# Scores in the free columns of the key banks, and a new order of stages, in an attention and feed-forward layer on one core

## The reference, cut to what matters

```python
h = layernorm(x) * (1 + ca) + sa                      # ca, sa, ga, sb, cb, gb come from a small matmul per sequence
q, k, v, g = h @ Wq.T, h @ Wk.T, h @ Wv.T, h @ Wg.T   # 8 heads; q, k 64 wide, v 128 wide, g 1024 wide
q, k = rotary(q), rotary(k)
o = (q @ k.T / 8 * decay[h] * causal) @ v             # decay[h] = gamma_h ** (t - s)
o = groupnorm_per_head(o) * gn_weight + gn_bias
x = x + ga * ((o * silu(g)) @ Wo.T)
h = layernorm(x) * (1 + cb) + sb
xr, xk = mixes of h with h one token before
x = x + gb * sigmoid(xr @ W_r.T) * (relu(xk @ W_k.T) ** 2 @ W_v.T)
```

## Time and profile before

| | us |
|---|---|
| median of three runs | 788.58 |
| the profiled execution | 789.72 |
| its span, first to last instruction | 787.8 |
| PE matmul busy | 753.8 (96%) |
| DVE, POOL, ACT busy | 597.4, 591.9, 443.1 |
| one group of four steps in the middle | 45.6 |

### The profile page before, as it was taken

How to read it: one execution, slowest core, us unless ns; L and a number is a source line. 1 busy time by engine, 2 the same in 40 slices (tenths; PEclk the granted TensorE clock), 3 DMA queues, 4 the chain that set the end, 5 groups by cost and what they waited for, 6 DMA issues and landing times.

```text
span 787.8 us, 29020 instructions
## 1 busy us (share of the span) xinstructions
PE 753.8 (96%) x12104; PEld 644.1 (82%) x12104; DVE 597.4 (76%) x1289; ACT 443.1 (56%) x799; POOL 591.9 (75%) x664
## 2 busy tenths in 40 slices
PE   4878999999999999999999999999999999999994
PEld 3667888888888888888888888888888888888783
DVE  5878888879777787877888797787878777776522
ACT  3324566646565655656566565656556565655672
POOL 4766878777878877877887777788778778775672
PEclk9889999999999999999999999999999999999997
DMA  9221222121212212221221222122122212212100
GB/s 305 44 44 39 42 42 43 30 42 36 54 30 63 42 40 53 55 49 37 62 42 43 53 52 50 35 63 42 40 56 53 53 31 50 42 36 49 29 14 27
DMA packets 63666, 39.60 MB, mean 50 GB/s; under 512 B 37936, under 2 KB 54448, under 8 KB 63408
## 3 DMA queue, kind: packets, MB, share of 16 engines
q1 hardware_dynamic: 62960, 36.92, 20.6%
q10 hardware_dynamic: 576, 0.83, 0.3%
HBM read 8.37 MB, written 4.19 MB: 16 GB/s over the span
## 4 chain that ended last, share of the span: by engine, by line
PE 90%; DVE 3%; issue 2%; POOL 2%; ACT 1%; DMA 1%; POOLq 0%; SPq 0%; DVEq 0%; ACTq 0%
PE ring L243 51%; PE outs L243 14%; PE O_E L243 13%; PE ring L258 8%; PE O_O L243 3%; PE ring L282 2%; DVE N L750 1%; DMA N<-in_w_qkT 1%; DVE gn_sum L739 1%; POOL y L883 1%; DVE swapped L695 1%; POOL gn_rstd L876 0%; POOL hT_lo L845 0%; ACT normed L484 0%; DVE turned L690 0%
## 5 line engine op out<-in xcount | busy, mean ns | idle before, releaser
L883 POOL TENSOR_TENSOR y<-y,gate 128x512 f32<-128x512 f32 x128 | 166.2, 1320 | 3.7 <-ACT y L524 3.7
L243 PEld LDWEIGHTS outs<-wo_gated,y 128*128 128x128 f32 x1024 | 132.1, 191 | 15.3 <-issue 7.0
L866 POOL TENSOR_TENSOR rot_k<-rot_k,sin_k 128x256 f32<-128x256 f32 x128 | 91.2, 735 | 67.8 <-DVE sin_k L712 67.8
L243 PE MATMUL outs<-wo_gated,y 128*128 128x128 f32 x1024 | 136.0, 276 | 0.1
L524 ACT ACTIVATE y<-ring,gn 128x512 f32<-128x512 f32 x128 | 98.8, 775 | 54.8 <-PE outs L243 28.9
L739 DVE TENSOR_REDUCE gn_sum<-squares 128x4 f32<-128x512 f32 x128 | 81.8, 680 | 42.1 <-ACT squares L512 41.2
L876 POOL TENSOR_TENSOR gn_rstd<-gn_var,minus_half 128x8 f32<-128x8 f32 x64 | 105.2, 1644 | 5.0
L709 DVE TENSOR_TENSOR rot_k<-ring,kcos 128x512 f32<-128x512 f32 x64 | 44.0, 688 | 79.5 <-PE ring L243 79.2
L512 ACT ACTIVATE squares<-O_O 128x512 f32<-128x512 f32 x64 | 38.2, 597 | 115.0 <-PE O_O L243 115.0
L517 ACT ACTIVATE gate<-ring 128x512 f32<-128x512 f32 x128 | 73.4, 597 | 29.9 <-PE ring L243 16.9
L860 POOL TENSOR_TENSOR qT<-qT,swapped 128x512 f32<-128x512 f32 x64 | 82.4, 1288 | 8.5 <-DVE swapped L695 8.5
(11 more groups left out here) (110 smaller groups left out, 2122.3 us busy)
## 6 DMA issues: line engine op xcount, KB each, us to landing
v<-v_odd SPq DMA_DIRECT2D x128, 128.0 KB, 2.3
k_odd<-rot_k SPq DMA_DIRECT2D x128, 64.0 KB, 2.2
X<-in_x SPq DMA_DIRECT2D x16, 256.0 KB, 3.1
out<-X SPq DMA_DIRECT2D x16, 256.0 KB, 2.6
rotary_q<-in_const_q SPq DMA_DIRECT2D x1, 1024.0 KB, 8.8
N<-in_w_qkT SPq DMA_DIRECT2D x1, 512.0 KB, 5.1
N<-in_w_vT SPq DMA_DIRECT2D x1, 512.0 KB, 6.7
N<-in_w_gT SPq DMA_DIRECT2D x1, 512.0 KB, 9.6
```

The costliest lines, as they stand in the source:

```text
L243: return e.matmul(o, lhsT, rhs, start=start, stop=stop, skip_group_check=True)
L866: done = e.tensor_tensor(turned[:, n, :, :], turned[:, n, :, :], sin[:, n, :, :], op)
L883: e.tensor_tensor(y[:, n % NY, :], y[:, n % NY, :], gate[:, n % 2, :], ALU.mult).then_inc(sem["y"])
```

## The change

1. `scores` takes no banks of its own. It writes into the columns 256 to 511 of the two banks that hold the same chunk's transposed keys; these banks are free again only when both masks have read the scores.
2. `turn_heads` stands at the head of the run of small tiles, directly in front of `transpose_k`, not at its end.
3. Every engine's list has a new order. On PE the two `project_out` stand next to each other, at the end of the full-size part; q, k, v and gates are one step earlier against the chunk's own step number, and so are the items of the other engines that go with them. The first step is -12, not -19; the earlier ones were empty on PE.
4. On SP, `swap_v` comes before `swap_k`, and both before `store` and the load of x. `store` of group g stands between the copies of chunk 4g+14 and those of chunk 4g+15. Before, it stood four steps further back, in front of the copies of chunk 4g+18.

```diff
             def transpose_k(i):
-                pair = take_two(("kT", i), ("kT", i + 1))
+                pair = take_two(("kT", i), ("A_E", i + 1), ("A_O", i + 1))
...
             def scores(i):
-                pair = take_bank(("A", 0, i), ("A_E", i + 1)), take_bank(("A", 1, i), ("A_O", i + 1))
...
-                        for odd, bank in enumerate(pair):
-                            done = matmul(bank[halves(half ^ odd), n * HALF:(n + 1) * HALF], kT[halves(odd), n, halves(half)],
-                                          queries(i, odd, n, half), True, True)
+                        for odd in range(2):
+                            bank = bank_of["kT", i][halves(half ^ odd), odd, W // 2 + n * HALF:W // 2 + (n + 1) * HALF]
+                            done = matmul(bank, kT[halves(odd), n, halves(half)], queries(i, odd, n, half), True, True)
...
             def mask(i, odd):
...
-                e.tensor_tensor(A[:, odd, :, :], by(PAIRS, bank_of["A", odd, i][:, 0:PAIRS * HALF]),
+                e.tensor_tensor(A[:, odd, :, :], by(PAIRS, bank_of["kT", i][:, odd, W // 2:W]),
```

and in SP's loop over the steps:

```diff
+                for i in due(step + 3, 1, NCHUNK):
+                    swap_v(i)
+                for i in due(step + 3, 1, NCHUNK):
+                    swap_k(i)
-                for g in due(step - 6, GC, NGROUP):
+                for g in due(step - 11, GC, NGROUP):
                     store(g)
...
-                for i in due(step + 12, 1, NCHUNK):
-                    swap_k(i)
-                for i in due(step + 12, 1, NCHUNK):
-                    swap_v(i)
```

More of the change, by code:

```diff
@@ L217, in loaded @@
             return "x%d" % (g % NX), 16 * (g // NX + 1)
-        steps = range(-19, NCHUNK + 11)
+        steps = range(-12, NCHUNK + 12)
         block = ctx.enter_context(nc.Block())
@@ L430, in _ @@
             for step in steps:
[L431 to L438, removed]
-                for i in due(step - 5, 1, NCHUNK):
[L440 to L458, removed]
+                for i in due(step - 6, 1, NCHUNK):
+                    project_out(2 * i + 1)
+                for i in due(step - 5, 1, NCHUNK):
+                    turn_heads(i)
                 for i in due(step, 1, NCHUNK):
@@ L468, in _ @@
                     state(i)
-                for i in due(step - 5, 1, NCHUNK):
-                    turn_heads(i)
+                for g in due(step - 12, GC, NGROUP):
+                    project_ffn_k(g)
+                for g in due(step - 14, GC, NGROUP):
+                    project_r(g)
+                for i in due(step + 1, 1, NCHUNK):
+                    project_v(i, 1)
+                for m in due(step + 4, 1, NCHUNK):
+                    project_q(m)
+                for g in due(step - 14, GC, NGROUP):
+                    project_ffn_out(g)
+                for i in due(step + 1, 1, NCHUNK):
+                    project_v(i, 0)
+                for i in due(step - 4, 1, NCHUNK):
+                    project_gate(2 * i)
+                for i in due(step - 4, 1, NCHUNK):
+                    project_gate(2 * i + 1)
+                for i in due(step + 2, 1, NCHUNK):
+                    project_k(i)
+                for i in due(step - 5, 1, NCHUNK):
+                    project_out(2 * i)
+                for b in due(step + 2, CB, B):
+                    mod_gates(b)
+                for g in due(step - 10, GC, NGROUP):
+                    transpose_n(g, 1)
+                for g in due(step + 5, GC, NGROUP):
+                    transpose_n(g, 0)
         @block.scalar
@@ L567, in _ @@
             for step in steps:
-                for i in due(step, 1, NCHUNK):
[L569 to L579, removed]
@@ L580, in _ @@
-                for g in due(step - 10, GC, NGROUP):
+                for i in due(step - 6, 1, NCHUNK):
+                    gate_silu(2 * i)
+                for i in due(step - 6, 1, NCHUNK):
+                    gate_silu(2 * i + 1)
+                for g in due(step - 12, GC, NGROUP):
+                    modulate2(g)
+                for i in due(step - 1, 1, NCHUNK):
+                    copy_kT(i)
+                for i in due(step - 6, 1, NCHUNK):
+                    scale_head(2 * i)
@@ new lines, in _ @@
+                for i in due(step - 6, 1, NCHUNK):
+                    scale_head(2 * i + 1)
+                for g in due(step + 3, GC, NGROUP, 1):
+                    round_h(g)
+                for i in due(step - 2, 1, NCHUNK):
+                    square(i, 0)
+                for i in due(step - 2, 1, NCHUNK):
+                    square(i, 1)
+                for g in due(step + 4, GC, NGROUP, 1):
+                    norm_apply(g, 0)
+                for g in due(step - 15, GC, NGROUP):
+                    act_r(g)
@@ L589, in _ @@
+                for i in due(step, 1, NCHUNK):
                     copy_v(i, 0)
[L590 to L597, removed]
         @block.vector
@@ L780, in _ @@
             for step in steps:
[L781 to L786, removed]
+                for g in due(step + 6, GC, NGROUP, 1):
+                    full_h(g)
+                for g in due(step + 9, GC, NGROUP, 1):
+                    norm_stats(g, 0)
+                for g in due(step - 7, GC, NGROUP):
+                    norm_stats(g, 1)
+                for b in due(step + 3, CB, B):
+                    mod_gates(b)
                 for g in due(step - 10, GC, NGROUP):
                     mix_shift(g)
[L789 to L812, removed]
                 for i in due(step + 2, 1, NCHUNK):
@@ L816, in _ @@
                     mask(i, 0)
+                for i in due(step + 1, 1, NCHUNK):
+                    sum_squares(i, 0)
+                for i in due(step + 1, 1, NCHUNK):
+                    sum_squares(i, 1)
+                for i in due(step + 2, 1, NCHUNK):
+                    add_state(i)
+                for m in due(step + 6, 1, NCHUNK):
+                    rotate_q(m)
+                for b in due(step + 4, CB, B):
+                    mod_input(b)
+                for i in due(step + 1, 1, NCHUNK):
+                    norm_heads(i, 0)
+                for i in due(step + 1, 1, NCHUNK):
+                    norm_heads(i, 1)
+                for g in due(step - 12, GC, NGROUP):
+                    ffn_product(g)
+                for i in due(step + 4, 1, NCHUNK):
+                    rotate_k(i)
+                for b in due(step - 4, CB, B):
+                    ffn_weights(b)
+                for g in due(step - 6, GC, NGROUP):
+                    residual(g)
         @block.gpsimd
@@ L909, in _ @@
             for step in steps:
+                for b in due(step, CB, B):
+                    gate_weights(b, 0)
+                for i in due(step - 2, 1, NCHUNK):
+                    gate_head(2 * i)
+                for g in due(step + 7, GC, NGROUP, 1):
+                    low_h(g)
+                for i in due(step - 2, 1, NCHUNK):
+                    gate_head(2 * i + 1)
+                for i in due(step + 2, 1, NCHUNK):
+                    head_rstd(i)
                 for g in due(step - 8, GC, NGROUP):
                     mix_delta(g)
[L912 to L917, removed]
+                for g in due(step + 9, GC, NGROUP, 1):
+                    norm_rstd(g, 0)
+                for g in due(step - 11, GC, NGROUP):
+                    ffn_out(g)
+                for c in due(step + 5, 1, CB, 1):
+                    key_tables(c)
+                for g in due(step - 6, GC, NGROUP):
+                    norm_rstd(g, 1)
                 for m in due(step + 7, 1, NCHUNK):
                     rotate_q(m)
[L920 to L926, removed]
+                for b in due(step - 2, CB, B):
                     gate_weights(b, 1)
```

17 lines of the change are left out of this document (4 added, 13 removed).

## The result

The changed kernel takes 800.94 us (median of 6 runs, 799.74 to 801.39), the one before 787.88 us (6 runs on the same chip, 787.08 to 789.14). The ratio is 1.0163, with a 95% interval of 1.0150 to 1.0176. The forecast of 783.3 us and its range up to 795 were wrong; so was the sign.

A forecast was written before the change was run, and what follows sets the result against it. PE, busy for 96% of the span, was taken to bound the kernel. The terms -9 - 4.9 + 8 + 1.6 - 1 = -5.3 us took the median of 788.6 to 783.3 us; range 773 to 795 us.

The forecast's parts named there:

- +8 us: SP's store waits for `ffn_out` ahead of chunk 4g+15's copies, so PE waits at the states: +8 us, bounds 0 to +20.
- the forecast's 7.5: PE's waits at the states in 12 steps, chunks 15 to 59: 6 x 0.85 + 6 x 0.4 = 7.5 us.
- For chunk 63 the wait hides: At chunk 63 the states' wait was to hide in the pipeline end's wait for N.
- upper bound of +20: Top of the range for the store holding up SP, if copies and store share the DMA engines badly: +20 us.
- -9 us, fewer layouts: Head and key transposes in one run on PE take 0.89 instead of 1.03 us in some 63 steps: -9 us.
- Rival C: The fused head and key transposes on PE save nothing: +9 us, 792.3 us; chance 0.08.
- -4.9 us, the gate's wait for `y`: PE's gate weight loads no longer wait for ACT's scaled heads: 0.19 x 26 = -4.9 us.
- rival B: PE's states wait for ACT's scaled heads in every step, 0.2 us in each of 56: +11, 794.5 us; chance 0.20.
- +1.6 us for `sin_k`: Key transposes wait for k's bank, left by DVE with `sin_k`, every second four-step cycle: 0.2 x 8 = +1.6 us.
- -1 us for fill and end: Fill unchanged in order; at the end, outputs one step closer to the heads: -1 us, bounds -4 and +4.
- Rival A: SP's copies land in time or `ffn_out` is earlier, so the +8 us is missing: 775.3 us; chance 0.20.
- Rival D: PE's pauses pull its clock down, 1.35 us after each of 12 pauses: +16, 799 us; chance 0.05.

The follow-up runs named there:

- experiment 5: The late store with the odd head's output moved between head and key transposes: 799.71 us, 19.1 us more than without this edit.
- the late store: Changed kernel with SP issuing each group's store three steps later, before the copies of chunk 4g+18: 780.62 us, 0.9912 of the kernel before.
- Experiment 6: The late store with the head transposes of chunks 61 to 63 moved ahead of the previous heads' output: 779.79 us, 0.9892 of the kernel before.

## Why the prediction was wrong, point by point

**The step that failed** is the term "**+8 us**" of the store that holds SP up. Its mechanism was right: the place, the frequency, the chain of engines. Its size was not: the twelve waits between the attends of chunks 4 and 60 add up to 18.7 us (0.85 to 2.04 each, taken as what the stage of the states lasts beyond its usual time), and the thirteenth, at chunk 63, is 1.45. What failed in it is the last stretch, from SP's issue of the copies to PE's first matmul: issue and landing were priced as in quiet steps, and from the landing to the matmul at nothing. By its own links, first for the group shown above, all counted from the first head transpose at 312.06 (the weight load's end, 0.07 ahead of the chain's 312.13):

- `X` predicted at 10.5, measured 322.59 - 312.06 = 10.5. The second k issued at 14.3, measured 14.15. Seven steps on four engines from rows of before came out within 0.15 us. In the other groups `X` starts at 10.5 to 10.8.
- Natural start of the states predicted at 15.7, measured 327.75 - 312.06 = 15.7. In every second group 0.45 more was predicted, for the gate matmuls, and 16.1 to 16.25 is measured. So this side was right.
- Landing predicted 2.2, measured 3.02 here. Of the 13 held steps, seven have 2.89 to 3.29 (3.12 on average) and six 2.17 to 2.28. That is 7 x 0.92 = 6.4 us. The 2.2 was a median over 128 issues, and in the kernel before nobody waited for those that land late.
- From the landing to PE's first matmul I put nothing; it is 0.24 or 0.25 in six of the twelve steps and 0.09 in the other six, those of every second group: 2.0 us.
- SP's second k issue comes at 14.15 to 14.4 in eight steps, but at 14.6 to 15.5 in four (chunks 31, 47, 51 and 55): one of the two issues of v took 0.8 to 1.8 us there, not 0.6. Together 3.2 us. The pair of v at chunk 31, against the same row at chunk 27:

```profile
324.38 1.13 SPq L962 DMA_DIRECT2D v<-v_odd  x2
...
371.13 2.21 SPq L962 DMA_DIRECT2D v<-v_odd  x2
```

- With the forecast's 7.5 these make 7.5 + 6.4 + 2.0 + 3.2 = 19.1, against 18.7 measured. The waits of every second group average 1.39 (1.22, 1.39, 1.59, 1.61, 0.85, 1.66), the others 1.72.
- "For chunk 63 the wait hides": it did not wholly. Last heads turned to last residual takes 22.6 us with the hold and without, but what comes ahead of it is 0.8 longer.

My upper bound of +20 held these twelve. What was wrong was to take "the middle because all its terms but one are rows": the rows of issue and landing were of quiet moments, they were the last links before PE, and each error behind the point where PE starts to wait counts in full.

**-9 us, fewer layouts.** Right. 0.89 us for heads and keys, as forecast; experiment 5 confirms the price from the other side. Rival C is out.

**-4.9 us, the gate's wait for `y`.** The wait is gone, and rival B's did not come: with the store out of the way no states wait for ACT's `y`. The margin was thin but held, since kT and the first scaling start 1.01 and 1.50 us after the first head transpose and the second is done at 2.94, where 1.00, 1.50 and 2.98 were reckoned (kernel with the late store, the run that starts at 305.81).

**+1.6 us for `sin_k`.** Missed: with the late store it appears once from 60 to 720 us, as 0.3.

**The middle together.** -0.14 x 56 - 4.9 + 1.6 = -11.1 was forecast between the two landmarks. With the late store it is 626.4 - 635.9 = -9.5 (attends at 74.21 and 700.57). The sum without the hold was right within 1.6 us, in part by luck, since the 1.6 for `sin_k` in it did not come. What takes some of the gain back is no seam but the choice of landmarks: the outputs come one step earlier, so that between the attends of chunks 4 and 12 PE has 128 output matmuls in the trace of the late store and 112 in the one of before, and 16 take 1.78 us. Between chunks 12 and 60 the counts are the same, and the change gains 550.3 - 539.8 = 10.5 us there, where 0.14 x 48 and at most 4.9 make 11.6. Its four-step period is 44.8 where 45.6 - 0.8 was forecast.

**-1 us for fill and end.** Wrong in sign at the end: +2.1 in the changed kernel, +1.9 with the late store, and that although the end has 16 output matmuls fewer now. The start shows nothing: it is +1.0 in the changed kernel and -1.3 with the late store, but -0.1 in the second profile of the same late store. The end (start us, us, what) of the changed kernel, against the earlier trace rows:

```profile
757.78 0.47 PE ring L258 x8
...
763.43 0.65 PE ring L258 x14
...
770.36 0.79 ACT y L523
...
777.83 1.28 POOL y L882
...
780.35 0.70 DVE X L754
```

The last link, gating to residual, is 2.5 us as before. But with outputs ahead of the heads' transposes each of the last rounds runs transposes, ACT, POOL, outputs one behind the other, and nothing is left to put beside them. Experiment 6, which turns the last heads earlier, has a shorter end and bears this out. I had counted the outputs that come earlier, not the heads that come later.

**Rival A** (no hold) did not happen. **Rival D** (clock) has 799, the nearest number, but not the cause: the granted clock's share is 1.00 from 60 to 720 us in spite of twelve such pauses. The Trainium skill (TensorE: Matmul & The Clock Gate, HAM oscillation) tells of a kernel throttled again and again by its waits between matmuls. These waits, at most 2.04 us long and one in some 46 us, did not do so.

Against the profiled span of before, 787.8: -9.5 in the middle without the hold, +18.7 for twelve holds, +1.0 and +2.1 at the ends are 800.1; the span is 799.6, so the account closes within 0.5 us. The forecast was -5.3 and the span grew by 11.8. Of the 17.1 between them 10.7 are the hold's, 1.6 the rest of the middle's, and some 5 lie at the two ends.

## What to carry to other kernels

A wait on a queue that only issues DMAs blocks all that stands behind it (11.7 us in all here). When an item is moved, list the items behind it and ask whose consumer has the least slack; the item itself may be harmless, as this store is (three steps later, or on another queue, it costs nothing and turns 1.016 into 0.991). And where a wait ends on a DMA, don't price its issue and landing by the median of copies that nobody waited for: look at the late ones among them, and let them set the end of the range.

## What the runs showed of the hardware

**Late landings.** In the changed kernel's seven held steps with a landing of 2.89 to 3.29 us, a packet of the instruction queue (q8, 16 KB) starts on one of the 16 DMA engines 0.3 to 0.4 us after the last copy is issued and takes 0.9 to 1.4 us there; in the six with 2.17 to 2.28 there is none in that time. The DMA view of the changed kernel from 326.2 to 329.3, where the landing is 3.02:

```profile
q1 hardware_dynamic: 1034, 0.48, 63.3%
q8 instruction: 1, 0.02, 1.9%
...
X<-in_x SPq DMA_DIRECT2D x1, 256.0 KB, 3.1
k_odd<-rot_k SPq DMA_DIRECT2D x1, 64.0 KB, 3.0
```

And from 374.0 to 376.3, where it is 2.21:

```profile
q1 hardware_dynamic: 693, 0.30, 68.0%
q14 instruction: 1, 0.01, 1.2%
...
X<-in_x SPq DMA_DIRECT2D x1, 256.0 KB, 3.1
k_odd<-rot_k SPq DMA_DIRECT2D x2, 64.0 KB, 2.2
```

The engines are about as busy in one as in the other, and the load of x, which SP issues 0.67 us behind the last copy in nine of the 13 steps, is in both: three of the landings on time have it, and one of the late ones (chunk 15, 2.89) has not. The version that waits without storing shows the same at its 13 held steps: in seven a packet starts 0.4 to 0.8 us after the issue and the landing takes 2.65 to 3.43 us, in six there is none and it takes 2.18 to 2.24. So the two go together in all 26 cases. They do so beyond the held steps: of the 64 last copies of k in the changed kernel, eleven have a packet starting between their issue and 0.9 us later and take 2.89 to 3.46, the other 53 take at most 2.58. With the late store only two of the 64 meet a packet so, and both are late (2.86 and 3.25), though it has as many packets. I take it that one part of the copy queues behind the 16 KB on its engine, but that is argued from the coincidence; no run took the packet away.

**Late issues.** The same packets go with SP's long issues. From 60 us on, 17 issues of the changed kernel took at least 0.15 us more than is usual for their kind (up to 1.87 us in place of 0.63), and a 16 KB packet of q8 overlaps every one. Among them are the issues of v in the four held steps of chunks 31, 47, 51 and 55. So in eleven of the twelve held steps such a packet goes with a late landing or a late issue. This too is a coincidence in time, and its cause isn't shown.

**A price for layouts.** Two changes between small and full tiles more per step cost 0.32 to 0.35 us. Joining heads and keys, which leaves one stage fewer to enter and leave, saved 0.14 (0.64 + 0.39 against 0.89).
